# A two-layer graph network on one core: 13 of 49 node blocks of the second layer summed from fetched rows instead of dense count products

## What is computed

```
h = relu(layernorm(x))
msg  = relu(h[src] + edge_attr @ W_edge.T + b_edge)
aggr = segment_sum(msg, dst)
x = x + relu(((1 + eps) * h + aggr) @ W1.T + b1) @ W2.T + b2      # first layer

h = relu(layernorm(x))
m = h[src] + 1e-7                                                 # second layer
a = softmax of m over the edges with the same dst, by feature
x = x + (h + segment_sum(a * m, dst)) @ W + b
```

## Time and profile before

| | us |
|---|---|
| median of three runs | 2489.45 |
| lowest, highest | 2484.88, 2493.21 |
| the profiled execution | 2481.58 |
| its span, first to last instruction | 2479.8 |

### The profile page before, as it was taken

How to read it: one execution, slowest core, us unless ns; L and a number is a source line. 1 busy time by engine, 2 the same in 40 slices (tenths; PEclk the granted TensorE clock), 3 DMA queues, 4 the chain that set the end, 5 groups by cost and what they waited for, 6 DMA issues and landing times.

```text
span 2479.8 us, 55001 instructions
## 1 busy us (share of the span) xinstructions
PE 1859.7 (75%) x11623; PEld 1549.9 (63%) x11624; DVE 1855.2 (75%) x4293; ACT 760.9 (31%) x1320; POOL 1513.4 (61%) x1559
## 2 busy tenths in 40 slices
PE   3777777767767767667767666767766778999999
PEld 2466656655656556556556555655655666888887
DVE  8999997878878888787878878878878885332333
ACT  5001121222223333334444444544544552000000
POOL 4777777777777777777777777777777712000000
PEclk9899898888888888888888888888888878999999
DMA  5234344444444454444445544544544527566563
GB/s 161 51 83 105 95 117 100 116 115 111 111 112 131 110 132 121 125 126 125 132 125 137 143 129 135 138 134 133 141 133 134 140 84 261 203 218 214 205 219 130
DMA packets 158402, 336.87 MB, mean 136 GB/s; under 512 B 65344, under 2 KB 115546, under 8 KB 142364
## 3 DMA queue, kind: packets, MB, share of 16 engines
q1 hardware_dynamic: 30944, 169.39, 22.7%
q0 software_dynamic: 49248, 75.74, 14.0%
q10 hardware_dynamic: 77990, 89.82, 10.7%
HBM read 244.91 MB, written 89.88 MB: 135 GB/s over the span
## 4 chain that ended last, share of the span: by engine, by line
POOL 54%; PE 20%; issue 18%; DVE 3%; DMA 1%; POOLq 0%; DVEq 0%; ACT 0%; ACTq 0%
POOL rows_buf L542 53%; PE ps L794 15%; DMA rows_buf<-table,index 1%; PE ps L620 1%; PE ps L630 1%; PE ps L722 1%; DVE zone L1311 1%; PE ps L820 1%; DVE planes L1076 0%; DVE ps L1274 0%; PE ps L808 0%; PE ps L776 0%; POOL planes L575 0%; PE ps L802 0%; POOLq L547 0%
## 5 line engine op out<-in xcount | busy, mean ns | idle before, releaser
L542 POOL DMA_INDIRECT rows_buf<-table,index x1539 | 1490.3, 968 | 496.0 <-issue 493.3
L722 PE MATMUL ps<-zone,planes 128*128 128x400 f16 x2352 | 612.6, 375 | 541.2 <-DVE zone L1311 438.7
L1311 DVE TENSOR_SCALAR zone<-iota_c,planes 128x400 f16<-128x400 int16 x2352 | 669.2, 338 | 58.3 <-issue 47.7
L722 PEld LDWEIGHTS ps<-zone,planes 128*128 128x128 f16 x2352 | 250.3, 107 | 721.0 <-issue 663.4
L929 ACT ACTIVATE features_buf<-ps 128x800 f16<-128x800 f32 x392 | 327.8, 836 | 1214.6 <-PE ps L722 1210.9
L620 PEld LDWEIGHTS ps<-wet,zone 128*128 128x128 f32 x3136 | 538.4, 246 | 40.2 <-issue 28.4
L620 PE MATMUL ps<-wet,zone 128*128 128x96 f32 x3136 | 527.1, 326 | 6.5 <-DMA zone<-edge_t 6.5
L607 PE MATMUL ps<-onehot,features_buf 128*96 128x128 f32 x3120 | 427.8, 283 | 0.0
L607 PEld LDWEIGHTS ps<-onehot,features_buf 128*96 128x96 f32 x3120 | 393.9, 173 | 11.9 <-issue 2.0
L1274 DVE TENSOR_TENSOR ps<-ps,rows_buf 128x768 f32<-128x768 f32 x171 | 164.5, 962 | 236.7 <-DMA rows_buf<-table,index 212.7
L1076 DVE TENSOR_TENSOR planes<-ps,planes 128x1536 f16<-128x1536 f32 x196 | 341.4, 1742 | 0.0
(11 more groups left out here) (163 smaller groups left out, 632.1 us busy)
## 6 DMA issues: line engine op xcount, KB each, us to landing
counts<-features_buf ACTq DMA_DIRECT2D x392, 200.0 KB
zone<-edge_t SPq DMA_DIRECT2D x98, 768.0 KB
rows_buf<-counts SPq DMA_DIRECT2D x32, 1600.0 KB, 6.2
single<-table SPq DMA_DIRECT2D x3072, 0.4 KB
planes<-counts SPq DMA_DIRECT2D x17, 1600.0 KB, 6.2
rows_buf<-table,index POOLq DMA_INDIRECT x1539
final<-residual ACTq DMA_DIRECT2D x48, 48.0 KB, 3.0
out<-final ACTq DMA_DIRECT2D x48, 48.0 KB, 3.5
```

The lines of the kernel that those rows point to most:

```text
L542: nc.gpsimd.indirect_dma_start(out=into[:, t, :], out_offset=None, in_=table, in_offset=bass.IndirectOffsetOnAxis(ap=at[:, t:t + 1], axis= ...
L722: nc.tensor.matmul(count_ps[:, bass.ds(banks[k], WC)], row_hot[:, u % 2, g * GS + k, :], pair_hot[:, g * GS + k, :], start=False, stop=Fal ...
L1311: last = nc.vector.tensor_scalar(pair_hot[:, k, :], iota_c[:, :], step_pair[:, bass.ds(i * (IS * SC) + (u * SC + k), 1)], None, ALU.is_equal)
```

## The change

Blocks 36 to 48 (GB = 13 of them) have 1679 to 2414 edges each in the reference's inputs. They are no longer summed from `counts`. Instead:

- SP writes `table16` out as a table `weighted` in memory, one row of 768 bytes a node, ten stores behind those of `hidden`.
- SP loads the src and dst of each of these blocks' edges, 26 loads whose addresses come from `block_start`. The starts are running sums of the edges by block, worked out by DVE and PE when the fast path is decided. The decision also asks whether each block's edges have room in FETCH, so many tiles of 128 edges.
- GpSimd gathers FETCH[g] tiles for block 36 + g, 242 in all, into one of two buffers, once `weighted` is stored and the block two fetches before is summed.
- DVE builds 242 one-hot matrices of 128 by 128, and PE makes 242 matmuls with them (`fetched_sums`) in the place of 13 x 50.
- ORDER mixes the two kinds: six dense blocks, the first fetched one, and from there a fetched one after every two or three dense ones; the last slot is block 48.
- The hardware loops of this stage are written out. Own rows and residual rows of a block share one semaphore, and the own rows of blocks 0 and 1 go out behind the stores of `weighted`.

```diff
+DB = 36
+GB = NB - DB
+FETCH = [20, 20, 20, 19, 19, 19, 19, 19, 18, 18, 18, 18, 15]
+LEAD = 6
+ORDER = []
+for d in range(DB):
+    ORDER.append(d)
+    ORDER.extend(DB + g for g in range(GB) if LEAD + 5 * g // 2 == d + 1)
...
# SP
+                sp.wait_ge(starts_ready, 1)
+                for g, start in enumerate(load(sp, block_start, DB, GB, [E] * GB)):
+                    n = FETCH[g]
+                    for buf, edge in ((fetch_src, edge_src), (fetch_dst, edge_dst)):
+                        sp.dma_start(buf[:, FETCH_AT[g]:FETCH_AT[g] + n],
+                                     edge[0:1, bass.ds(start, P * n)].rearrange("a (p k) -> (a p) k", k=n)
+                                     ).then_inc(fetch_in, 16)
                 for u in range(NU):
                     sp.wait_ge(features, NU + u + 1)
...
+                for u in range(NU):
+                    sp.wait_ge(exp_high, u + 1)
+                    sp.wait_ge(exp_low, u + 1)
+                    sp.wait_ge(weighted_high, u + 1)
+                    sp.wait_ge(parts_ready, u + 1)
+                    for part in (slice(0, EVEN), slice(EVEN, NP)):
+                        sp.dma_start(weighted.rearrange("(p j) d -> p j d", j=NJ)[part, units[u], :],
+                                     table16[part, units[u], :]).then_inc(weighted_out, 16)
                 sp.wait_ge(own_out, 2 * NU * 16)
                 sp.wait_ge(step_done, SC + NSTEP)
                 for b in range(2):
-                    sp.dma_start(own[:, b, :], hidden[b * P:(b + 1) * P, :]).then_inc(own_in[b], 16)
+                    sp.dma_start(own[:, b, :], hidden[b * P:(b + 1) * P, :]).then_inc(residual_in[b], 16)
...
+                for b in range(3, DB):
+                    sp.wait_ge(block_ps, 2 + ORDER.index(b - 3) + 1)
+                    block_load(b)
...
# GpSimd
+                pool.wait_ge(fetch_in, 2 * GB * 16)
+                pool.wait_ge(own_out, 2 * NU * 16)
+                pool.wait_ge(weighted_out, 2 * NU * 16)
+                for g in range(GB):
+                    if g >= 2:
+                        pool.wait_ge(block_ps, 2 + ORDER.index(DB + g - 2) + 1)
+                    gather(fetched[g % 2], weighted, fetch_src[:, FETCH_AT[g]:FETCH_AT[g + 1]], fetched_in[g % 2], FETCH[g])
...
# PE
-            pe.wait_ge(bad_ready, 2)
-            nc.tensor.transpose(ps[0:1, 6, 0:P], bad[:, 2:3], ident[:, :]).then_inc(bad_ps, 1)
+            pe.wait_ge(bad_ready, 3)
+            nc.tensor.transpose(ps[0:1, 6, 0:P], bad[:, 2:3], ident[:, :])
+            nc.tensor.matmul(ps[0:1, 6, P:P + NB], ones[:, 0:1], in_block[:, :], start=True, stop=True)
+            nc.tensor.matmul(ps[0:NB, 7, 0:1], in_block[:, :], ones[:, 0:1], start=True, stop=True).then_inc(bad_ps, 1)
...
+                def fetched_sums(s, g):
+                    pe.wait_ge(fetched_in[g % 2], fetched_before(g + 2))
+                    pe.wait_ge(fetch_hot_done, g + 1)
+                    pe.wait_ge(soft_done, s + 1)
+                    for k in range(FETCH[g]):
+                        last = nc.tensor.matmul(ps[:, s % 2, 0:4 * D], fetch_hot[g % 2][:, k, :],
+                                                fetched[g % 2][:, k, :], start=(k == 0), stop=(k == FETCH[g] - 1))
                     last.then_inc(block_ps, 1)
...
+                for s in range(2, NB):
+                    if ORDER[s] < DB:
+                        block_sums(s, ORDER[s])
+                    else:
+                        fetched_sums(s, ORDER[s] - DB)
+                    turn(s - 1, s - 1)
+                    finish(s - 2, s - 2)
...
# DVE
+                def fetch_hots(g):
+                    dve.wait_ge(fetch_at_ready, g + 1)
+                    if g >= 2:
+                        dve.wait_ge(block_ps, 2 + ORDER.index(DB + g - 2) + 1)
+                    for k in range(FETCH[g]):
+                        last = nc.vector.tensor_scalar(fetch_hot[g % 2][:, k, :], iota_c[:, 0:P],
+                                                       fetch_at[:, FETCH_AT[g] + k:FETCH_AT[g] + k + 1], None,
+                                                       ALU.is_equal)
+                    last.then_inc(fetch_hot_done, 1)
...
+                for s in range(2, NB):
+                    for g in range(GB):
+                        if ORDER.index(DB + g) == s + 2:
+                            fetch_hots(g)
+                    softmax(s, s, 0)
+                    add_aggregate(s - 1, (s - 1) % 2)
+                    add_final(s - 2, s - 2, 0, min(P, N - ORDER[s - 2] * P))
```

More of the change, by code:

```diff
@@ L68 @@
 FEAT = 5760
+DB = 36
+GB = NB - DB
+FETCH = [20, 20, 20, 19, 19, 19, 19, 19, 18, 18, 18, 18, 15]
+FETCH_AT = [sum(FETCH[:g]) for g in range(GB + 1)]
+LEAD = 6
[3 more added lines that the diff above has]
+    ORDER.extend(DB + g for g in range(GB) if LEAD + 5 * g // 2 == d + 1)
+assert len(ORDER) == NB
+EPAD = P * max(FETCH)
 NE = 4
 NW2 = 2
-FIRST = 2
-LAST = FIRST + (NB - FIRST) // BU * BU
 NWIN = NB * BW
@@ L116, in gnn_kernel @@
     residual = nc.dram_tensor("residual", (N, D), F32, kind="Internal").ap()
+    weighted = nc.dram_tensor("weighted", (N, 4 * D), F16, kind="Internal").ap()
     hidden = nc.dram_tensor("hidden", (N, D), F32, kind="Internal").ap()
@@ L343, in gnn_kernel @@
         own_out = sem("own_out")
-        own_in = [sem(f"own_in{u}") for u in range(BU)]
         residual_in = [sem(f"residual_in{u}") for u in range(BU)]
@@ L386, in by_tile, with fetched_before @@
             return buf.bitcast(dt).rearrange("p (q e) -> p q e", q=QT)
+        def fetched_before(g):
+            return 16 * sum(FETCH[g % 2:g:2])
         t1 = table1.rearrange("(p j) d -> p j d", j=NJ)
@@ L1010, in _ @@
[L1010 to L1016 removed]
+                for s in range(BU - 2):
+                    residual_load(s)
@@ L1017, in _ @@
+                for s in range(NB):
+                    n, rows_at = rows_of(s)
+                    act.wait_ge(final_ready, s + 3)
+                    act.dma_start(out[rows_at, :], final[0:n, s % BU, :]).then_inc(final_out[s % BU], 16)
+                    if s + BU - 2 < NB:
+                        if s >= 2:
+                            act.wait_ge(final_out[(s - 2) % BU], ((s - 2) // BU + 1) * 16)
+                        residual_load(s + BU - 2)
                 for u in range(BU):
@@ L1432, in _, with fetch_places @@
                 product_rest(4)
+                def fetch_places():
+                    dve.wait_ge(fetch_in, 2 * GB * 16)
+                    for g in range(GB):
+                        at = slice(FETCH_AT[g], FETCH_AT[g + 1])
+                        nc.vector.tensor_scalar(fetch_at[:, at], fetch_dst[:, at], float((DB + g) * P), None,
+                                                ALU.subtract).then_inc(fetch_at_ready, 1)
+                def fetch_hots(g):
[7 more added lines that the diff above has]
+                    last.then_inc(fetch_hot_done, 1)
                 def softmax(b, u, i):
@@ L1551 @@
     dst_tiles = tiles(dst, QT * P, NPAD)
+    flat = {k: np.full((1, E + EPAD), pad, np.int32) for k, pad in (("src", 0), ("dst", NPAD))}
+    flat["src"][0, :E] = np.asarray(src)
+    flat["dst"][0, :E] = np.asarray(dst)
     arrays = {
```

133 lines of the change are left out of this document (63 added, 70 removed).

## The result

| | us |
|---|---|
| kernel before, median of four runs (lowest, highest) | 2487.16 (2482.57, 2493.21) |
| changed kernel, median of four runs (lowest, highest) | 4275.28 (4254.57, 4276.83) |
| changed kernel, profiled execution and its span | 4276.77, 4275.0 |

The ratio is 1.7168, 95% interval 1.7101 to 1.7234. The forecast was 2427.5 us in a range of 2415 to 2460, so it is wrong by 1848 us and in sign.

What follows compares the result with a forecast made beforehand. The prediction took GpSimd's gathers to bound the first layer and PE the second layer's 47 blocks; -66.3 + 3.7 + 0.7 = -61.9 us, applied to a median of 2489.45, gave 2427.5 us, range 2415 to 2460.

Steps and rivals of the forecast that it cites:

- The step that failed: Rival at the decision: fast path not taken for lack of room in FETCH, adding 1568 gathers, 2000 us; chance 0.01.
- PE's sum: Second layer, blocks 36 to 48: 242 matmuls replace 13 x 50, 66.3 us less.
- DVE's one-hots: Second layer: 242 one-hots at 0.17 us each, 3.2 us for 19, hidden in DVE's idle time.
- GpSimd's gathers: Second layer: 242 gathers of 768-byte rows at 1.27 us each, 308 us, ending before PE wants the last block.
- one-hots that block: Rival in the second layer: each one-hot holds a gather up, 1.44 to 1.51 us a gather, 2456 to 2473 us; chance 0.14.
- wide rows that are slow: Rival on GpSimd's queue from 2079.5 us: gathers up to 2.21 us, 2635 us, slower than before; chance 0.09.
- DMA share: Second layer: block loads plus gathers take 0.68 to 0.85 of the DMA engines, below full; nothing added for block loads.
- The test's 1 us: Fast-path test before the node layer: one more reduction and small operations, everything behind it 1 us later.
- The start: Start of the second layer: PE goes on at 2079.6 instead of 2075.89 us, 3.7 us later; bounds 1 and 10.
- SP's 26 loads: SP's queue before the stores: loads with addresses from registers take 12 us, from 2046 to 2058.
- The stores and the own rows behind them: SP's queue: 7.2 MB at 423 GB/s take 17 to 18 us from 2058.5, own rows land at about 2079.
- The first layer: Stage up to about 2000 us, paced by GpSimd's gathers: taken as untouched by the change, no time added.

Runs made afterwards that it cites:

- e7: e1 with block starts worked out and SP's 26 loads issued earlier, and own rows of blocks 0 and 1 fetched by ACT: 2445.78 us, ratio 0.9833.
- e8: e1 without its 242 gathers, the one-hots multiplied with table16 instead: 2436.71 us (one run).
- e5: e1 with the table weighted, the buffers and gathers typed as 192 float32, the same bytes a row: 2453.94 us (one run).
- e4: Kernel before with 240 narrow gathers added in the second layer that feed nothing, some indices padding: 2570.85 us, ratio 1.034.
- e1: Changed kernel with one number altered, the test's room for block 48 raised by 704; fast path taken: 2458.83 us, ratio 0.9899.
- e2: Changed kernel with 18 instead of 15 tiles for block 48; fast path still refused: 4273.14 us (one run).
- e3: Changed kernel with 19 instead of 15 tiles for block 48; fast path taken: 2464.9 us (one run).
- f1: Kernel before, unchanged, traced on a chip of slow pace: 3647.15 us.
- f4: Kernel before with 16 narrow gathers added behind GpSimd's last work, on a slow chip: 3653.99 us beside 3647.48 of the kernel before.
- f3: Kernel before with 224 narrow gathers added, 192 in a hardware loop, on a slow chip: 3903.32 us beside 3647.48 of the kernel before.

## Why the prediction was wrong, point by point

**The step that failed** is in the rivals: "The room in FETCH must hold the edges of each block. Counted from the reference's inputs, blocks 36 to 48 hold 1679 to 2414 edges, and the tightest leaves 85 free places." It had 0.01. The count was right and of the wrong thing. The test compares what the kernel has put into `counts`, and that includes 704 padding edges, all in block 48. By real edges that block has 241 places to spare and is not the tightest; as the kernel counts it is 463 over. The price of that rival, 1568 gathers at 1.27 us, was near: 1.30 each. The sum did not matter beside it.

**PE's sum** of -66.3 us was right. Measured -64.5, which holds 2.1 us for block 2's matmuls, which began at a granted clock of 0.50 (10.41 instead of 8.34 us), where I had 0 to 1.6.

**DVE's one-hots**: 0.17 us each as forecast (20 in 3.43 us; the single record is 0.24 us). Hidden as forecast.

**GpSimd's gathers**: 1.26 us against 1.27, no wait of PE for them. The two rivals about them, one-hots that block and wide rows that are slow, did not happen. DMA share 0.74, inside 0.68 to 0.85.

**The test's 1 us**: its reduction took 0.53 us and lies in the first stretch; the node layer then took its 35.8 us as before.

**The start** was mis-sized: 3.7 us forecast with the test's 1 us, 10 as the bound, 18.2 measured. Two steps of it were short. SP's 26 loads took 20.3 us against 12, two of them beside full DMA engines. The stores and the own rows behind them took 26.6 us against 20.5: they were the limit that I had named, but at 270 GB/s, the rate of my bound, and not at 423, which I had read off a load at another place than I wrote (2026 us, not 2042). The bound of 10 us had the slow stores without the slow loads. That the own rows stood behind the stores of `weighted` in SP's queue was right, and e7 shows it: on ACT's queue PE waits 1.4 us.

**The first layer** had no term, and it cost more than the start, 26.1 us. "The change touches the second stage alone" was the sentence for it. e8, e5 and e4 show that the second stage's gathers do it; through what is open. With both terms put in as measured the same sum gives 2479.8 - 66.3 + 18.2 + 26.1, about 2458 us, where e1's span is 2459.6. So even with the fast path taken the forecast of 2427.5 us would have been 31 us too low, half of the gain.

## What to carry to other kernels

A guard that compares counts must be checked against the numbers as the kernel forms them, padding included, before any term of a time is worked out; its price here, 1788 us, was some thirty times the 62 us that the rest was to bring. When a queue gets more DMAs, price its issuing and its bytes, and take the rate from a row of the same kind: here SP's loads cost 8 us more than forecast and the stores, priced by a load, 6 us. And a gain that rests on gathers from GpSimd beside a busy PE should be timed on more than one chip, and at more than one time.

## What the runs showed of the hardware that I had not expected

- Gathers on the fast path of the second layer lengthen the first layer's, 940 to 951 ns at the least, on two chips (e2 against e1 and e3; e8 against e4, e5 and e7), and with sixteen of them already 942 to 949 on another (f1, f4); the general path with its 1568 does not (e2).
- On three chips the kernel before took 3640 to 3710 us instead of 2485. In f1 SP needs 15 to 40 us for 32 single loads instead of 15, while the second layer without gathers takes 396 us at either pace.
- In f3 PE did 104 matmuls in 280 us while GpSimd issued 199 gathers, and 2013 in 320 us (3560 to 3880 us) without them.
- The stores of `weighted` filled the DMA engines (share 0.98) at 318 GB/s in e1, where the loads of blocks 1 and 2 and the store of `residual` filled them (1.04) at 391.
- A gather of 128 rows takes GpSimd the same 0.96 us for 384 (e4) and for 768 bytes a row (e1).
